# Transformer layer on 8 cores: LayerNorm rows and V blocks of attention transposed by SP's DMA queue too, with that queue's loads and stores in another order

## The reference

```
x = x + attn(layernorm(x))          # attention among the 16 heads of ONE token
x = x + ffn(layernorm(x))

def attn(x):
    qkv = einsum('bnm,fm->bnf', x, Wqkv).reshape(b, n, 16, 192)
    q, k, v = the three 64-wide parts
    scores = einsum('bnhd,bngd->bnhg', q, k) / 8     # 16 x 16 for each token
    out = einsum('bnhg,bngd->bnhd', softmax(scores), v)
    return out.reshape(b, n, 1024) @ Wproj.T + bproj

def ffn(x):       # bitlinear: activations rounded to 8 bits by row, weights to -1, 0, 1 times a mean
    return bitlinear(silu(bitlinear(x, w_gate)) * bitlinear(x, w_up), w_down)   # inner width 4096
```

## Time and profile before

| | us |
|---|---|
| median of 3 runs | 4117.74 (3936.12 to 4165.67) |
| the profiled execution | 3933.93 |
| its span, core 7, the slowest | 3932.4 |
| its span, core 3, the shortest | 3898.9 |
| mean granted TensorE clock, core 7 / core 3 | 0.989 / 0.993 |

### The profile page before, as it was taken

How to read it: one execution, slowest core, us unless ns; L and a number is a source line. 1 busy time by engine, 2 the same in 40 slices (tenths; PEclk the granted TensorE clock), 3 DMA queues, 4 the chain that set the end, 5 groups by cost and what they waited for, 6 DMA issues and landing times.

```text
span 3932.4 us, 88522 instructions; the slowest of 8 cores (3898.9 to 3932.4 us)
## 1 busy us (share of the span) xinstructions
PE 3812.5 (97%) x36034; PEld 2097.5 (53%) x36034; DVE 2256.2 (57%) x3800; ACT 878.6 (22%) x1474; POOL 256.0 (7%) x386
## 2 busy tenths in 40 slices
PE   6999999999999899999999999999999999999999
PEld 5777777777775344444444444444444444444444
DVE  2433456676675656555565565555555655555554
ACT  2555643333342111111111111111111111111110
POOL 1111112121110000000000000000000000000000
PEclk9999999999999999999999999999999999999999
DMA  9667556656645332222222322222222222222221
GB/s 196 185 196 212 187 177 201 181 162 191 200 149 178 97 60 58 58 62 52 60 60 51 62 60 57 62 52 60 59 52 62 58 57 61 54 60 60 51 62 49
DMA packets 427535, 393.97 MB, mean 100 GB/s; under 512 B 348480, under 2 KB 354880, under 8 KB 426560
## 3 DMA queue, kind: packets, MB, share of 16 engines
q1 hardware_dynamic: 387536, 266.66, 26.8%
q0 software_dynamic: 39600, 121.66, 11.7%
HBM read 230.96 MB, written 79.69 MB: 79 GB/s over the span
## 4 chain that ended last, share of the span: by engine, by line
PE 95%; issue 2%; DMA 2%; DVE 0%; DVEq 0%; ACT 0%; SPq 0%; POOL 0%; ACTq 0%; POOLq 0%
PE pb L513 22%; PE pb L486 22%; PE pb L498 22%; PE pb L388 17%; PE pb L467 6%; PE pb L370 1%; PE pb L447 1%; PE pb L390 1%; PE pb L429 1%; PE pb L411 1%; DMA wqkv_sb<-wqkvT 1%; DMA x_ln<-x 1%; PE pb L404 0%; PE pb L472 0%; DMA xq_fm<-xq_tm 0%
## 5 line engine op out<-in xcount | busy, mean ns | idle before, releaser
L486 PE MATMUL pb<-wg,xq_fm 128*128 128x512 fp8e4 x4096 | 970.4, 380 | 12.0 <-DMA xq_fm<-xq_tm 11.7
L498 PE MATMUL pb<-wu,xq_fm 128*128 128x512 fp8e4 x4096 | 968.5, 379 | 0.0
L513 PE MATMUL pb<-wd,hq_fm 128*128 128x512 fp8e4 x4096 | 965.0, 379 | 0.0
L794 DVE SCALAR_TENSOR_TENSOR m<-pb,agm,silug 128x512 f32<-128x512 f32 x512 | 384.2, 750 | 950.1 <-PE pb L498 946.8
L621 ACT ACTIVATE silug<-pb,agm 128x512 f32<-128x512 f32 x512 | 351.8, 687 | 2286.3 <-PE pb L486 2286.2
L388 PE MATMUL pb<-xn_fm,wqkv_sb 128*64 128x256 bf16 x6144 | 753.6, 279 | 20.2 <-DMA wqkv_sb<-wqkvT 10.5
L390 PE MATMUL pb<-xn_fm,wqkv_sb 128*64 128x256 bf16 x6144 | 754.7, 279 | 7.8 <-issue 7.8
L388 PEld LDWEIGHTS pb<-xn_fm,wqkv_sb 128*64 128x64 bf16 x6144 | 658.5, 112 | 79.6 <-issue 56.0
L486 PEld LDWEIGHTS pb<-wg,xq_fm 128*128 128x128 bf16 x4096 | 400.8, 98 | 496.9 <-issue 16.6
L498 PEld LDWEIGHTS pb<-wu,xq_fm 128*128 128x128 bf16 x4096 | 401.1, 98 | 484.3 <-issue 1.7
L390 PEld LDWEIGHTS pb<-xn_fm,wqkv_sb 128*64 128x64 bf16 x6144 | 658.6, 112 | 1.0 <-issue 1.0
(11 more groups left out here) (77 smaller groups left out, 2012.0 us busy)
## 6 DMA issues: line engine op xcount, KB each, us to landing
x_ln<-x SPq DMA_DIRECT2D x64, 512.0 KB, 7.0
stage<-wgT POOLq DMA_DIRECT2D x64, 512.0 KB, 5.6
x_res<-x SPq DMA_DIRECT2D x64, 512.0 KB, 10.8
xnew_scr<-x_res SPq DMA_DIRECT2D x64, 512.0 KB, 5.8
stage<-wuT POOLq DMA_DIRECT2D x64, 512.0 KB, 5.0
stage<-wdT POOLq DMA_DIRECT2D x64, 512.0 KB, 4.7
xnb<-xnew_scr SPq DMA_DIRECT2D x64, 512.0 KB, 4.5
out<-outb SPq DMA_DIRECT2D x64, 512.0 KB, 2.6
```

The lines of the kernel that those rows point to most:

```text
L486: ins = t.matmul(PG[jg % 2][:], xq_fm[k % 2][:, m * 128:(m + 1) * 128], wg_sb[pc][:, m * 512:(m + 1) * 512], start=(m == 0), stop=(m == 7))
L498: ins = t.matmul(PU[jg % 2][:], xq_fm[k % 2][:, m * 128:(m + 1) * 128], wu_sb[pc][:, m * 512:(m + 1) * 512], start=(m == 0), stop=(m == 7))
L513: ins = t.matmul(PD[pcd][:], hq_fm[k % 2][:, m * 128:(m + 1) * 128], wd_sb[q][:, (m - 8 * q) * 1024 + pcd * 512:(m - 8 * q) * 1024 + (pcd ...
L794: STT(ms, PU[jg % 2][:], agm[:, 2 * (k % 2) + 1:2 * (k % 2) + 2], silug[jg % 2][:], ALU.mult, ALU.mult).then_inc(SM["v_m"], 1)
```

## The change

TensorE and ScalarE no longer transpose xn of tiles 1 to 15 and V of tiles 0 to 14. SP does, with 8 DMA transposes a tile: `xn_transpose(it+1, s)` in slots 13 to 16, each behind a wait for `xn_tm[s]`, and `v_transpose(it-1, q)`, four in slot 0, behind a wait for the last V eviction of the tile. Tile 0's xn and tile 15's V stay on TensorE. SP's other DMAs move: the four `load_ln` of a tile go to slot 16, behind the xn transposes; `load_res` of sub-blocks 0 and 1 stays in slot 18, that of 2 and 3 goes from slot 22 to slot 3 of the next tile (in the last tile it stays). QKV waits for `s_xnT`, attention-times-V for `s_vT0` or `s_vT1`; the wait for the quantization scales goes from the V transposes to the first projection.

```diff
-XNT_SLOT = {17: (0,), 18: (1,), 19: (2,), 20: (3,), 21: (4, 5), 22: (6, 7)}
...
+            def xn_transpose(t, s):
+
+                sync.wait_ge(SM["v_xn"], 4 * t + s + 1)
+                if t >= 2 and s == 0:
+                    sync.wait_ge(SM["t_qkv"], 24 * (t - 1))
+                dst = xn_fm[t % 2][:].rearrange("p (m t) -> p m t", m=8)[:, :, s * 128:(s + 1) * 128]
+                sync.dma_start_transpose(out=dst, in_=xn_tm[s][:]).then_inc(SM["s_xnT"], 16)
+
+            def v_transpose(a, q):
+
+                if q == 0:
+                    sync.wait_ge(SM["a_qkv"], 24 * (a + 1))
+                    if a >= 1:
+                        sync.wait_ge(SM["t_AV"], 4 * a)
+                cols = slice(q * 1024, (q + 1) * 1024)
+                sync.dma_start_transpose(out=v_th[:, cols].rearrange("p (m t) -> p m t", m=8),
+                                         in_=v_sb[:, cols]).then_inc(SM[f"s_vT{q // 2}"], 16)
...
+                    if 1 <= it < nt and c == 0:
+                        for q in range(4):
+                            v_transpose(it - 1, q)
...
-                    if it + 2 < nt and c in (14, 15):
-                        for s in ((0, 1) if c == 14 else (2, 3)):
+                    if it + 1 < nt and 13 <= c < 17:
+                        xn_transpose(it + 1, c - 13)
+                    if it + 2 < nt and c == 16:
+                        for s in range(NSUB):
                             load_ln(it + 2, s)
-                    if 1 <= it < nt and c in (18, 22):
-                        for s in ((0, 1) if c == 18 else (2, 3)):
+                    if 1 <= it < nt and c == 18:
+                        for s in (0, 1):
+                            load_res(it, s)
+                    if 2 <= it < nt and c == 3:
+                        for s in (2, 3):
+                            load_res(it - 1, s)
+                    if it == nt - 1 and it >= 1 and c == 22:
+                        for s in (2, 3):
                             load_res(it, s)
...
             def qkv(it, c):
...
-                if c == 0:
-                    t.wait_ge(SM["a_xnT"], 8 * (it + 1))
+                if it == 0 and c == 0:
+                    t.wait_ge(SM["a_xnT"], 8)
+                if it >= 1 and c == 0:
+                    t.wait_ge(SM["s_xnT"], 64 * it)
...
             def av(a, pr, half):
...
-                t.wait_ge(SM["a_Vt"], 8 * a + 4 * pr + 4)
+                if a + 1 < nt:
+                    t.wait_ge(SM[f"s_vT{pr}"], 32 * (a + 1))
+                else:
+                    t.wait_ge(SM["a_Vt"], 4 * pr + 4)
...
             def proj(a, half, pc):
...
+                if a + 1 == n1 and half == 0 and pc == 0:
+                    t.wait_ge(SM["v_scale"], 1)
...
-                    if it >= 1 and c < 4:
-                        vT(it - 1, 2 * c)
-                        vT(it - 1, 2 * c + 1)
...
-                    if it + 1 < nt and c in XNT_SLOT:
-                        for g in XNT_SLOT[c]:
-                            xnT(it + 1, g)
...
             def qkv_ev(it, c):
...
                 if it >= 1 and c == 16:
-                    sc.wait_ge(SM["t_Vt"], 8 * it)
+                    for pr in range(2):
+                        sc.wait_ge(SM[f"s_vT{pr}"], 32 * it)
...
             def apply(tt, s):
...
-                if tt >= 1:
-                    v.wait_ge(SM["t_xnT"], 8 * (tt - 1) + 2 * s + 2)
+                if tt == 1:
+                    v.wait_ge(SM["t_xnT"], 2 * s + 2)
+                if tt >= 2:
+                    v.wait_ge(SM["s_xnT"], 64 * (tt - 1))
```

More of the change, by code:

```diff
@@ L126, in build_nc @@
             "a_abs", "t_sum", "v_scale", "v_q",
-            "g_zero", "v_st1", "g_rs1", "v_xn", "t_xnT", "a_xnT", "t_qkv", "a_qkv",
+            "g_zero", "v_st1", "g_rs1", "v_xn", "t_xnT", "a_xnT", "s_xnT", "s_vT0", "s_vT1", "t_qkv", "a_qkv",
             "t_S", "v_s1", "a_exp", "v_pT", "t_Vt", "a_Vt", "t_AV", "a_AV", "v_AV", "t_pj", "v_pe",
@@ L363, in xnT @@
                 t.wait_ge(SM["v_xn"], 4 * tt + s + 1)
-                if tt >= 2 and g < 2:
-                    t.wait_ge(SM["v_pe"], 8 * (tt - 1))
                 if tt * 8 + g >= 2:
@@ L418, in vT @@
                     t.wait_ge(SM["a_qkv"], 24 * (a + 1))
[L419 to L422, removed]
+                    t.wait_ge(SM["v_pe"], 8 * a)
                 if g >= 2:
-                    t.wait_ge(SM["a_Vt"], 8 * a + g - 1)
-                if g == 1 and a + 1 == n1:
-                    t.wait_ge(SM["v_scale"], 1)
+                    t.wait_ge(SM["a_Vt"], g - 1)
                 for i in range(4):
@@ L456, in proj @@
                     t.wait_ge(SM["s_bias"], 32)
-                if half == 0 and pc == 0:
-                    t.wait_ge(SM["a_Vt"], 8 * (a + 1))
-                else:
+                if a + 1 == nt and half == 0 and pc == 0:
+                    t.wait_ge(SM["a_Vt"], 8)
+                if a + 1 == n1 and half == 0 and pc == 0:
+                    t.wait_ge(SM["v_scale"], 1)
+                if a >= 1 or half == 1 or pc == 1:
                     t.wait_ge(SM["v_pe"], 8 * a + 4 * half + 2 * pc)
@@ L526, in tensor_body @@
                         t.wait_ge(SM["a_abs"], NQ)
+                        if it >= 2:
+                            t.wait_ge(SM["v_pe"], 8 * (it - 1))
                         t.matmul(P[5][:, 0:NQ], c_ones[:], acc_sb[:], start=True, stop=True).then_inc(SM["t_sum"], 1)
-                    if it >= 1 and c < 4:
-                        vT(it - 1, 2 * c)
-                        vT(it - 1, 2 * c + 1)
                     if it >= 1 and c in AV_SLOT:
@@ L595, in vT_ev @@
             def vT_ev(a, g):
-                sc.wait_ge(SM["t_Vt"], 8 * a + g + 1)
+                sc.wait_ge(SM["t_Vt"], g + 1)
                 if a >= 1 and g == 0:
@@ L628, in scalar_body @@
                     qkv_ev(it, c)
-                    if it >= 1 and c < 4:
-                        vT_ev(it - 1, 2 * c)
-                        vT_ev(it - 1, 2 * c + 1)
                     if it >= 1 and c in AV_SLOT:
@@ L637, in scalar_body @@
                         expo(it, 0, c - 21)
-                    if it + 1 < nt and c in XNT_SLOT:
-                        for g in XNT_SLOT[c]:
-                            xnT_ev(it + 1, g)
                     if n0 <= it < n1:
@@ L857, in vector_body @@
                     if it == nt - 1 and c == 4:
-                        v.wait_ge(SM["t_xnT"], 8 * nt)
+                        v.wait_ge(SM["s_xnT"], 64 * (nt - 1))
                         ln_stats(0)
@@ L873, in vector_body @@
                 if pc == 4:
-                    v.wait_ge(SM["t_Vt"], 8 * nt)
+                    v.wait_ge(SM["t_Vt"], 8)
                     ln_stats(1)
```

## The result

The changed kernel takes 3955.81 us (median of 6 runs, 3948.98 to 4050.18) against 3933.44 for the kernel before beside it. The ratio is 1.0066, with a 95% interval of 1.0041 to 1.0091: 26 us slower, where 3872 (1.6% faster) was forecast and 3945 was the end of the range. The profiled execution took 3952.26 us, span 3950.7 on core 1, granted clock 0.981 (0.989 before on its slowest core).

What follows compares the result with a forecast made beforehand. TensorE's instruction order was taken to bound the kernel. From 3933.93 us, a running gain of 73, plus 5 for tile 1 and 6 for fetches, gave 3872 us (ratio 0.984), range 3820 to 3945.

Steps and rivals of the forecast that it cites:

- What bounds it: Whole kernel: TensorE's instruction order sets the end, busy 97% of the span; instruction fetches likely cause attention's "issue" waits.
- (1): Attention tiles: without xn and V transposes TensorE's order loses 4.5 us a tile, 68 us in all, upper bound 84.
- (2): Attention tiles: waits on ScalarE's evictions of the removed blocks go too, 5 us, at the least 0.
- (3): Attention tiles: SP's DMA transposes land 4.4 us after issue and cause no wait; xn hidden even at 12.5.
- V hidden: T: end of last v_sb eviction; V pairs land by T + 8.3, slack 3.2 and 4.9 us, no wait.
- rival C: Attention tiles: gain partly lost, by later fetches or V landing after 12.5 us (74 us); 3905 to 3946, chance 0.18.
- (4): Tile 1: V transposes queue behind the 2 MB wproj copy; attention-times-V waits, cost 3 to 7 us, taken as 5.
- (5): Attention tiles: DMA share rises from 0.63 to 0.83, delaying TensorE's instruction fetches; +6 us, bounds -10 to +15.
- rival B: Score slots: loads and stores leave their second half, fetches come in time, clock stays up; 3839, chance 0.20.
- D: Attention tiles: larger fetch delay makes it slower, deciding from 0.35 us a block; 4022 at 0.8 us; chance 0.08.
- C's first branch: Attention tiles: fetches come 0.2 us later on each of 13 blocks a tile, 39 us, giving 3905.

Runs made afterwards that it cites:

- e6: Kernel before, all transposes on TensorE, with the four x_ln loads held by a wait for the last xn_tm block so they go in one burst; ratio 1.0036.
- e10: Kernel before with all four x_res loads of a tile held back by a wait until slots 1 and 4 of the next tile; ratio 0.9919.
- e15: Kernel before with the x_res loads held back by a wait until slots 1 and 7 of the next tile; ratio 0.9874.
- e4: Changed kernel with the DMA transposes left out (xn after tile 1, V of tiles 1 to 14), later tiles using old data; ratio to before 0.994.
- e7: Changed kernel with V back on TensorE and each xn transpose replaced by a plain copy of the same 256 KB; ratio to before 1.0004.
- e13: Changed kernel with V back on TensorE and xn transfers left out from tile 2 on, later tiles using old xn_fm; ratio to before 0.9976.
- e3: Changed kernel with xn back on TensorE and SP's old load order, only V by DMA transposes; ratio to before 1.0029.
- e14: Changed kernel with xn on TensorE, SP's old order, V transfers left out from tile 2, wproj copy behind tile 1's; ratio to before 0.996.
- e1: Kernel before with only SP's new written order of loads, all transposes on TensorE; ratio 0.9992.
- e2: Changed kernel with V back on TensorE, only xn by DMA transposes, new order of loads; ratio to before 1.0051.

## Why the prediction was wrong, step by step

**What bounds it: right.** TensorE in attention; the FFN didn't move (2688 us from its first gate matmul to the end, both). The cause named for the "issue" waits, fetches behind data, is borne out by the runs that moved data and nothing else (e6, e10, e15), and by the waits' ends, 1.1 to 1.7 us after a block landed. The Trainium skill ("Runtime: NRT & Kernel Launch", Instruction fetch mechanics) says that a 16 KB crossing is mostly hidden. By count this case agrees: 26 waits over 0.5 us for 172 blocks before. But the prediction's reading of it, that then fetches can't be the cause and data can't lengthen the waits, fails: the same instructions had 43.5 us of these waits before and 16.1 us in e15.

**(1) The work removed: right, 10 us small.** 78.4 us measured, 68 predicted (bound 84).

**(2) Eviction waits: right.** 5 us taken; the waits on the removed evictions were 3.4 us by the mean of the cores.

**(3) xn hidden: right from tile 2 on**, by the landing of 6.6 us at the median. **V hidden: the step that failed first.** "VectorE is next in line but 4.3 us early" takes the softmax's block for av (1, 0) (the third of the tile, ready at T + 8.9 against T + 13.2) as VectorE's last word. But av (1, 0) also waits for VectorE's eviction of av (0, 0), with 1.2 us of slack in the rows of before, and VectorE's order doesn't move forward when TensorE's does. Of the 2.2 us a tile (33 in all) that V's matmuls gave up there, 17.9 us stood again as attn_fm waits, and 22.6 with all transfers left out (e4). The V blocks' landing came on top: 11.7 us. The transposes of after on SP (issue ns min/median/max, landing), V and then xn:

```profile
L210 SPq DMA_TRANSPOSE v_th<-v_sb x60: 1222/1526/12582, 95.7 to 1187.6; - x60
...
DMA to landing us min/median/max: 3.1/5.2/27.3
```

```profile
L201 SPq DMA_TRANSPOSE xn_fm<-xn_tm x60: 1217/2251/9215, 55.6 to 1156.6; - x60
...
DMA to landing us min/median/max: 3.5/6.6/29.3
```

4.4 us was taken for the landing, from a single transfer. 5.2 is the median here, and SP needs 1.5 us in place of 1.2 for each issue. By tile (mean of 8 cores) the first pair, forecast 5.6 us after the first issue, lands after 6.1 to 6.8 us in tiles 8 to 14, which the slack of 3.2 us covers, and after 8.2 to 10.2 in tiles 2 to 6, which it doesn't. There GpSimd's weight loads had half of the DMA engines' time in slots 0 to 4 already before the change (50%; 18% in tiles 8 to 14), the likely reason, not tested by a run of its own. The rows that the slack was read from are of one tile of the second kind (704 us). The waits are of up to 4.2 us, and not the 74 us of rival C.

**(4) Tile 1: 23 us in place of 5.** SP and TensorE on core 1:

```profile
85.55 6.91 SPq L201 DMA_TRANSPOSE xn_fm<-xn_tm  x1
92.56 2.43 SPq L187 DMA_DIRECT2D x_ln<-x  x4
95.08 0.54 SPq L267 DMA_DIRECT2D wproj_sb<-wproj_sb  x1
95.71 28.27 SPq L210 DMA_TRANSPOSE v_th<-v_sb  x4
```

```profile
123.99 1.04 PE L474 MATMUL pb<-pT,v_th 32*64 32x32 bf16 x64 [14.98 <-DMA v_th<-v_sb]
```

The mechanism was as written, the transposes behind the 2 MB copy, but the copy's 13.8 us was its landing on a quieter queue. Now four x loads stand ahead of it, and the four transposes' issue alone takes 28 us. The xn blocks of tile 1, the first to be transposed by SP, are late as well (9.1 us by the mean), a wait that the prediction had hidden.

**(5) Fetches: +6 predicted, +33.5 in waits measured, and +25 in low clock, to which the other waits give their part.** This is the largest error. The DMA share was forecast well (0.83; 0.85 came), and the step went wrong behind it: it let delay grow with the mean share, and said that "xn transposes land mostly before the scores" and that "two of four x_res loads leave the score slots". Both came true and didn't help. The transposes do land mostly before, but SP's queue is one line, and the x loads that stood behind them ran on through the score slots to slot 22: 20 of the 33.5 us lie in slots 18 to 23. The two x_res loads did leave, and with the V transposes ahead of them they fell into slots 4 to 6, around two attention slots, where the instructions are densest: another 11 us in slots 4 to 8. e7 shows the first part with plain copies, e13 puts 14 us on the missing matmuls and 27 on the transfers, e10 and e15 undo it from the other side, and they show the second part too (13.5 us in slots 4 to 8 with the loads in slot 4, 3.7 in slot 7). V's transposes by themselves, at as large a share, cost next to none (e3 45.7, e14 45.5; 5 us in slots 4 to 8), presumably since they run mostly in QKV slots. The low clock was in the prediction only as a possible gain (rival B). Short waits of 1 to 4 us were followed by half clock, so each us of new gaps cost a further 0.3 us (25 over 82), and not through fetches alone: e3, with "issue" as in before, has 36 us more of gaps than before and 58.3 us at half clock in place of 40.5.

**The rivals.** The outcome, slower, is D's, which was given 0.08, but not by D's mechanism alone. Over the prediction's 195 blocks 33.5 us are 0.17 us a block, and 0.30 with all of the low clock, under D's break-even of 0.35; the 0.17 is nearly the 0.2 of C's first branch. Even with all the low clock put down to it, 33.5 + 25 = 58.5 us would leave 20 of the 78 us gained; the V chain (16.4 + 11.7 = 28) and tile 1 (23) turn the sign. C and D had been weighed as alternatives to the forecast, and a fetch term of C's size came together with two terms that had been put at 0 and 5.

## What to carry to other kernels

Time taken off the engine that bounds is worth only the slack of the next instruction's other waits; list all of them, not just the one whose data moves, and leave the removed work out altogether (as e4 does) before building what replaces it. Instruction fetches share the DMA engines with data: keep transfers out of the stretches with the most instructions per us, by a wait that really holds the queue, since a queue that nothing gates runs ahead of its written order (e1). In the kernel before, that alone (four loads a tile moved, behind two waits) gave 1.3%. And read a slack in more than one tile: the late V blocks came in tiles 2 to 6, and the forecast rested on rows of a later one.

## What the hardware showed beyond that

- Issuing a DMA transpose of 128x1024 bf16 held SP for 1.22 us when the queue was free, 2.25 us at the median for xn, and up to 12.6 us under load.
- The transposes hold SP's queue longer than copies of the same bytes (on core 5, 2.08 us an issue at the median in e2 and 0.47 in e7; the queue's share of the DMA engines from 150 to 1150 us is 37.5 and 28.2%), but delay TensorE's fetches little more (85.6 and 80.4 us).
- An "issue" wait of TensorE ends 1.1 to 1.7 us after a 16 KB instruction block has landed (94 to 99% of those over 0.5 us). The block's own transfer takes the same with few and with many such waits: 0.98 us at the median in before, 1.02 in after, 0.97 in e15. So a late block starts late; its transfer isn't slower.
- What makes a fetch start late, and behind which of the transfers, no run here shows. Only the slots in which data lies were shown to matter.
